# Projecting fourteen blocks among the first layer's gathers, building the first block's cells ahead of pass 1, and spreading the read-back of a table

## The reference

```
edge_index = stack([src, dst])
x = layernorm(x + L0(x, edge_index, weight, attn_l, attn_r))   # attention over 4 heads
x = layernorm(x + L1(x, L1_W, edge_index))                     # h = x @ W;  sum of d[src] d[dst] h[src]
x = layernorm(x + L2(x, edge_index, edge_weight, W1, b1, W2, b2))  # two such layers, weighted
x = layernorm(x + L3(x, W, edge_index))                        # h = x @ W.T
# L0: alpha = softmax(leaky_relu(alpha_l + alpha_r)); out = sum over heads of alpha * (x @ weight)[dst]
```

## Time and profile before

| | |
|---|---|
| median of three runs | 3285.67 us (3281.23 to 3291.87) |
| profiled execution, its own time | 3282.31 us, span 3280.5 us |
| gather loop and preparations | 0 to 151.7 us |
| first table | to 223.4 us, first gather of pass 1 at 227.37 us |
| pass 1 | 230.3 to 1364.7 us (first and last product of a chunk) |
| PE, DVE, ACT, POOL busy | 94%, 69%, 54%, 60% of the span |
| granted clock of PE, mean | 0.977 |

### The profile page before, as it was taken

The page is one execution under the profiler, slowest core; times in us unless marked ns, Lnnn a source line. Parts: engine busy times, 40 slices in busy tenths (PEclk is TensorE's granted clock), DMA queues, the critical chain, the costliest instruction groups (busy, mean ns, idle before and its releaser), DMA issues.

```text
span 3280.5 us, 58762 instructions
## 1 busy us (share of the span) xinstructions
PE 3072.6 (94%) x18902; PEld 2516.0 (77%) x18902; DVE 2278.6 (69%) x8972; ACT 1770.7 (54%) x4797; POOL 1974.7 (60%) x1952
## 2 busy tenths in 40 slices
PE   6788999999999997799999999899999998999998
PEld 5666777777877776578888887788888876888887
DVE  6668999999999997477777777466666673322333
ACT  3555878878878876444444444344444453232222
POOL 6627777777777776577777777577777770000000
PEclk9888999999999998899999999899999999999999
DMA  6246878878877878667767665766767666444443
GB/s 204 76 178 197 256 239 251 256 244 255 260 243 248 260 244 275 222 200 219 212 214 213 209 213 173 265 215 212 214 211 216 211 198 218 159 153 137 156 170 119
DMA packets 338323, 690.01 MB, mean 210 GB/s; under 512 B 61814, under 2 KB 185532, under 8 KB 337114
## 3 DMA queue, kind: packets, MB, share of 16 engines
q1 hardware_dynamic: 244506, 433.77, 39.1%
q0 software_dynamic: 91568, 250.58, 27.0%
q10 hardware_dynamic: 1936, 1.84, 0.2%
HBM read 495.15 MB, written 190.82 MB: 209 GB/s over the span
## 4 chain that ended last, share of the span: by engine, by line
PE 71%; DVE 10%; DMA 10%; POOL 3%; ACT 3%; issue 2%; SPq 1%; ACTq 0%; DVEq 0%
PE PS L2100 24%; PE PS L2177 15%; PE PS L2146 7%; DMA G<-T,idx 6%; PE PS L2148 6%; PE PS L2054 4%; PE PS L1895 2%; POOL G L2248 2%; PE PS L2027 2%; PE PS L1896 2%; PE PS L2078 2%; DVE soh L1481 2%; PE PS L2114 1%; DVE M L1363 1%; DVE R L1372 1%
## 5 line engine op out<-in xcount | busy, mean ns | idle before, releaser
L2248 POOL DMA_INDIRECT G<-T,idx x1800 | 1853.5, 1030 | 639.3 <-issue 257.5
L2100 PE MATMUL PS<-H,aw 128*128 128x256 f32 x4214 | 1078.5, 382 | 12.3 <-DMA aw<-AW 8.0
L2100 PEld LDWEIGHTS PS<-H,aw 128*128 128x128 f32 x4214 | 789.7, 191 | 129.0 <-issue 8.8
L1723 ACT ACTIVATE R<-G,wD 128x256 fp32r<-128x256 f32 x990 | 500.4, 508 | 699.7 <-PE PS L2148 482.4
L1372 DVE SCALAR_TENSOR_TENSOR R<-G,wD,R 128x256 fp32r<-128x256 f32 x990 | 480.6, 485 | 373.3 <-ACT R L1723 369.3
L2148 PE MATMUL PS<-R,Mr 128*128 128x512 f32 x990 | 575.6, 583 | 24.1 <-DVE R L1372 22.7
L2146 PE MATMUL PS<-G,M 128*128 128x257 f32 x1620 | 522.0, 406 | 48.6 <-DMA G<-T,idx 44.7
L2177 PE MATMUL PS<-HH,cr 128*128 128x512 f32 x2205 | 501.4, 389 | 0.4 <-DVE cr L1560 0.3
L2177 PEld LDWEIGHTS PS<-HH,cr 128*128 128x128 f32 x2205 | 413.3, 188 | 88.4 <-DVE cr L1560 2.6
L1781 ACT CAST atp<-PS 128x512 bf16<-128x512 f32 x588 | 336.2, 575 | 123.7 <-PE PS L2027 95.7
L2146 PEld LDWEIGHTS PS<-G,M 128*128 128x128 f32 x1620 | 266.0, 194 | 84.4 <-DMA G<-T,idx 32.1
(11 more groups left out here) (252 smaller groups left out, 3980.6 us busy)
## 6 DMA issues: line engine op xcount, KB each, us to landing
aw<-AW SPq DMA_DIRECT2D x301, 448.0 KB, 3.6
AT<-atp SPq DMA_DIRECT2D x539, 128.0 KB
br<-AT SPq DMA_DIRECT2D x77, 896.0 KB, 4.8
AW<-awp SPq DMA_DIRECT2D x264, 256.0 KB
G<-T,idx POOLq DMA_INDIRECT x1800
AT<-atf SPq DMA_DIRECT2D x49, 256.0 KB
T<-tst SPq DMA_DIRECT2D x96, 128.0 KB
H<-T SPq DMA_DIRECT2D x12, 896.0 KB, 12.0
```

Of the source, the lines that this page charges most:

```text
L1723: e.activation(R[m % NR][:, 0:D], G[slot][:, 0:D], ACT.Copy, scale=wD[:, k // NC, k % NC:k % NC + 1]).then_inc(s_rw, 1)
L2100: ins = e.matmul(ps, aw[n_ % NAW][:, s_ % 7, :], H[:, s_, :], start=s_ == 0, stop=s_ == NBK - 1)
L2248: e.indirect_dma_start(G[slot][:, 0:D], None, TAB[p][0:N, :], bass.IndirectOffsetOnAxis(ap=idx[:, block_of(p, k), k % NC:k % NC + 1], axis ...
```

## The change

It has three parts. (1) In the gather loop, from iteration 28 on, fourteen of the 49 blocks (`AMONG`) are turned and projected among the gathers, in six slots for turned tiles (two are lent from `counts1`) instead of four. The first five products (`NRAW`) come before `d1` is known, so ACT stores them unscaled and scales them at iterations 38 to 42 (`scale`). Counters of turns and products are now looked up (`TURN0`, `PRODUCT0`). The windows, digits and degrees sit two to twelve iterations earlier; a fifth group is early (five groups, 35 blocks), and 14 blocks are `LATE`; POOL normalizes 14 blocks instead of 10. (2) The cell sort of the first built block leaves pass 1: DVE has it (`BUILD0`) behind its first-layer work, PE and ACT around the last projections; `FIRST_PAIR` falls from 28 to 6, so pairs are spread over 798 chunks instead of 776, and the sort of the second block starts at chunk 0. (3) The six reloads with a due chunk had 739, 739, 739, 739, 739 and 755; now they have 738, 750, 762, 774, 786 and 798.

```diff
-PERM, FIRST_PAIR, LAST_PAIR = 9, 28, 6
+PERM, FIRST_PAIR, LAST_PAIR = 9, 6, 6
-ROW_AT, WINDOW_AT, TURN_AT = 3, 8, (14, 15, 16)
-DIGIT_AT = (22, 23, 24, 25, 26, 27, 28)
-DEGREE_AT, ROOT_AT = 37, 44
-EARLY_AT = ((7, 14, 18), (24, 36, 39), (37, 43, 46), (45, 48, 48))
+ROW_AT, WINDOW_AT, TURN_AT = 3, 8, (11, 12, 13)
+DIGIT_AT = (20, 21, 22, 23, 24, 25, 26)
+DEGREE_AT, ROOT_AT = 31, 32
+EARLY_AT = ((7, 14, 18), (20, 32, 34), (33, 39, 44), (34, 44, None), (39, None, None))
+AMONG = {28 + 10 * x // 7: x for x in range(14)}
+NRAW, SCALE_AT = 5, 38
...
-SHARED = list(LATE)[1::2]
+BEHIND = [g for g, at_ in enumerate(EARLY_AT) if at_[2] is None]
+SHARED = list(range(GROUPS[BEHIND[0]], NBK))[1::2]
...
-    ready = [(0, b) for b in range(LATE[0])]
+    ready = [(0, b) for b in range(len(AMONG), LATE[0])]
...
+    S_ += [(0, ("build", "dup", 0)), (k - 7, ("build", "totals", 0)), (k + 9, ("build", "cells", 0))]
+    T_ += [(k - 8, ("build", "totals", 0)), (k - 5, ("build", "rank", 0))] + [(k + 8, ("build", "permute", 0, c)) for c in range(NC)]
...
+BUILD0 = [("cellhot", 0), ("pieces",), ("pick", 0), ("pack", 0), ("over", 0), ("less", 0), ("slots", 0), ("load", 0),
+          *(("place", 0, c) for c in range(NC))]
...
             early_group(1, 1)
-            digit_sums(NBK // DB - 1)
             early_group(2, 0)
-            early_group(1, 2)
-            early_group(2, 1)
             w.wait_ge(s_ds, 1)
...
+            early_group(1, 2)
             w.wait_ge(s_sqd, 1)
             for i in range(4):
                 newton("d1n", i, d1[:, :], degI[:, :], [t_[:, :] for t_ in rt])
...
+            early_group(3, 0)
+            early_group(2, 1)
+            early_group(4, 0)
             early_group(3, 1)
+            early_group(2, 2)
+            early_group(4, 1)
             early_group(3, 2)
-            for _, step in FIRST[EARLY][0]:
+            for _, step in FIRST[EARLY][0][:16]:
+                first(step)
+            early_group(4, 2)
+            for _, step in FIRST[EARLY][0][16:]:
                 first(step)
...
+            for step in BUILD0:
+                behind_(step)
             for p in (1, 2, 3):
                 aggregate(p)
...
                 if b >= 1:
                     first_rows(b - 1)
+                if b - 1 in AMONG:
+                    follow(0, ("multiply", AMONG[b - 1]))
+                if b in AMONG:
+                    follow(0, ("turn", AMONG[b]))
...
+            free = UNITS1[-1][-1] + 4
+            reload_at = [max(free + r * (chunks_of(1) - free) // 6, *(stored[b] + 4 for b in blocks_in(r))) for r in range(6)]
...
-                                         + [(max(UNITS1[-1][-1], *(stored[b] for b in blocks_in(r))) + 4, (reload2, r)) for r in range(6)]):
+                                         + [(reload_at[r], (reload2, r)) for r in range(6)]):
```

More of the change, by code:

```diff
@@ L157, in follow_late @@
         k = put("soft", EARLY, i)
-    S_.append((k + 1, ("exp", EARLY)))
+    S_.append((4, ("exp", EARLY)))
+    for n, g in enumerate(BEHIND):
+        if EARLY_AT[g][1] is None:
+            S_.append((8, ("root", g)))
+        S_ += [(9 + 18 * n + 3 * i, ("normalize", b)) for i, b in enumerate(range(GROUPS[g], GROUPS[g + 1])) if b not in SHARED]
     for i in range(3, 6):
         put("soft", EARLY, i)
-    ready = [(0, b) for b in range(LATE[0])]
+    ready = [(0, b) for b in range(len(AMONG), LATE[0])]
     stages = ("mul", "mix", "sum", "stat", "aggr")
@@ L201, in first_early, with first_order @@
     for g, (e, r, n) in enumerate(EARLY_AT):
-        out[r].append(("root", g))
+        if r is not None:
+            out[r].append(("root", g))
         out[e].append(("exp", g))
-        for i, b in enumerate(range(GROUPS[g], GROUPS[g + 1])):
-            out[min(n + i, NBK - 1)].append(("normalize", b))
+        if n is not None:
+            for i, b in enumerate(range(GROUPS[g], GROUPS[g + 1])):
+                out[min(n + i, NBK - 1)].append(("normalize", b))
+    for b in range(NRAW):
+        out[SCALE_AT + b].append(("scale", b))
     return out
 FIRST_EARLY = first_early()
+def first_order():
+    turns, products = [], []
+    for b in range(NBK):
+        turns += [("edge", 2 * b), ("edge", 2 * b + 1)]
+        if b >= 1:
+            products.append(("rows", b - 1))
+        if b - 1 in AMONG:
+            products.append(("table", AMONG[b - 1]))
+        if b in AMONG:
+            turns.append(("table", AMONG[b]))
+    products.append(("rows", NBK - 1))
+    for _, (kind, b, *_) in FIRST[EARLY][2]:
+        if kind != "build":
+            (turns if kind == "turn" else products).append(("table", b))
+    return turns, products
+TURNS0, PRODUCTS0 = first_order()
+TURN0, PRODUCT0 = ({x: i for i, x in enumerate(order)} for order in (TURNS0, PRODUCTS0))
+NX0 = 6
 def chunks_of(p):
@@ L1656, in first @@
             def first(step):
-                kind, b = step
-                if kind == "exp":
+                kind, b = step[0:2]
+                if kind == "build":
+                    behind_(step[1:])
+                elif kind == "exp":
                     w.wait_ge(s_v, at["soft", b, 2])
@@ L1825, in aggregate @@
                     follow(p, step)
+            for _, step in FIRST[EARLY][1]:
+                first(step)
+            w.wait_ge(s_wt, 1)
+            w.wait_ge(s_pj, PRODUCT0["rows", NBK - 1] + 1)
+            e.copy(W4[:, 0, 0:D], PT[:, 0:D])
+            e.copy(W4[:, 1, 0:D], PA[1][:, 0:D]).then_inc(s_w4, 1)
             for p in (1, 2, 3):
@@ L2161, in aggregate @@
                     follow(p, step)
+            for _, step in FIRST[EARLY][2]:
+                if step[0] == "build":
+                    behind_(step[1:])
+                else:
+                    follow(0, step)
+            w.wait_ge(L["W4"], 16)
+            w.wait_ge(s_xt, turn_at(2, 0))
+            for i in range(2):
+                for j in range(2):
+                    ins = e.transpose((PT, PA[1])[i][:, j * P:(j + 1) * P], W4r[:, j, i * P:(i + 1) * P], ident[:, :])
+            ins.then_inc(s_wt, 1)
             for p in (1, 2, 3):
```

141 lines of the change are left out of this document (75 added, 66 removed).

## The result

The changed kernel takes 3265.85 us (median of 12 runs, 3261.0 to 3276.6), the kernel before 3284.82 in the same comparison; the ratio is 0.9953 with a 95% interval of 0.9938 to 0.9968. So it is faster, but by 19 us between the medians, and by 15 (10 to 20) by the ratio, where 43 were forecast, and the time lies just outside the range of 3220 to 3264. In three of the six comparisons of this document every kernel took 13 to 15 per cent longer (the kernel before 3712 to 3763 us instead of 3279 to 3285), so times and stages are set beside each other only at the same level. The profiled execution took 3262.61 us with a span of 3260.8.

A forecast was written before the change was run, and what follows sets the result against it. PE, busy 94% of the span, was taken as the bound, so only its idle or waiting stretches could give time. 3282.3 - 20 - 15 - 6 = 3241 us, with the runs' median 3.4 higher; stated as 3242, range 3220 to 3264.

The forecast's parts named there:

- PE needs 21 x 1.71 = 35.9: Gather loop from iteration 28 to 48: PE's own work at 1.71 us an iteration, 35.9 us.
- 15.1 us for the blocks: Gather loop: PE's work for the 14 blocks moved in, 14 x 1.08 us.
- My 4.4 us for the clock: Gather loop: 51 us of PE work take 4.4 us more at a clock of 0.92.
- The waits were forecast at 7.6: Gather loop: 5.6 us for turns waiting on ACT and 2 us for ACT's table switches.
- my bound of 168: Latest loop end, if every table switch and a whole trip to ACT count; 160 us was forecast.
- Rival C: In the loop ACT waits for DVE at iterations 39 and 44; loop ends at 172, total 3254 us; chance 0.10.
- 22 chunks of 1.350 instead of 1.25 us: Start of pass 1, chunks 6 to 27: each goes from the gather's pace to 1.350 us with pairs there.
- rival B: Parts 1 and 3 act, but pass 1's pace isn't set by the build: 3261 us; chance 0.10.
- half of 3 each: End of pass 1: six single reloads cost between 0 and 18 us, taken as 9, against 15.4 before.
- rival D: Spreading the reloads gives nothing back, six stalls of 3 us; 32 us gained in all, 3252 us; chance 0.05.
- Rival F: Slower: late DVE results hold up ACT's queue in the loop; 3290 us if DVE is 48 us late; chance 0.05.
- E: Total within 0.3%, if part 1 is lost in the loop and one other part too; chance 0.05.

The follow-up runs named there:

- rows_half_2: Changed kernel without the second wide product of first_rows in loop iterations 28 to 48, at the shorter times: 3255.2 us, ratio 0.9930 to the kernel before.
- the second comparison: Changed kernel, unedited, measured again against the kernel before at 3281.7 us: 3267.5 us, ratio 0.9967.
- pair17: Changed kernel with FIRST_PAIR 17 instead of 6: ratio 0.9960 to the kernel before, which took 3711.9 us there.

## Why the prediction was wrong

**Part 1, 20 us forecast, 6.3 measured.** The step that failed is "PE needs 21 x 1.71 = 35.9". The 1.71 us were the distance of two turns in one place, in which PE did nothing else and ran at full clock; the row that counts is the window of the same 54.1 us, in which PE was busy 47.44 us, 2.26 an iteration. Split in two, that window of the kernel before shows a start at half clock:

```profile
97.60:106.30 8.70, 8.65 (x47) 7.88 (x48) 8.70 (x28) 2.00 (x8) 6.71 (x7) 0.50 0.35 106
106.30:151.70 45.40, 38.79 (x255) 33.69 (x254) 25.92 (x94) 30.94 (x97) 35.72 (x61) 1.00 0.32 96
```

The rest of the difference is, as far as it is known, some 3 us of products for the digits and degrees and a 22nd group of products in the window; about 3 us are not accounted for. With the 15.1 us for the blocks 47.44 makes 62.5, and the changed kernel shows 62.88. My 4.4 us for the clock made up part of it; 35.9 + 15.1 + 4.4 = 55.4 was 7 short. The waits were forecast at 7.6 and came to 72.5 - 62.9 = 9.6. So the loop ended at 170.1, beyond my bound of 168. Behind the loop 47.6 us passed instead of 43.6: PE was busy 43.66 there, just the forecast, and the 3.9 us of idle time, the 2.04 us wait for ACT among them, were not in it. The 4.0 us from the last block to the first gather held.

One sum over the rows would have stopped the forecast: from 97.6 to 223.4 us PE did 47.44 + 0.31 + 57.82 = 105.6 us of work, which the change only moves. An end at 203.6 left PE 0.4 us of idle time in the whole stretch. In fact its idle time went from 20.2 to 13.6 us (120.1 less 62.9 and 43.7) and its busy time from 105.6 to 106.5, which makes the 5.7 us by which the stretch is shorter. That PE's work is what the forecast lacked agrees with rows_half_2, where less of it made the loop shorter.

Rival C had the loop's end nearly right (172) and the cause wrong. ACT came to iteration 39 straight from a normalize, without a wait for DVE; PE waited for the two table loads. From the rows of iteration 38 to those of 39 it took 6.1 us, where its neighbours took 2.5 to 4.1, and it took the same 6.1 us in rows_half_2 with less work for PE. The loads were 1.28 us each, and the activations followed 10 and 20 ns behind: no drain here either, where the Trainium skill ("ScalarE: Activation LUTs", What ACT_TABLE_LOAD costs) has 1.38 us.

**Part 2, 15 forecast, 6.9 measured.** Two terms were mis-sized. The start was put at 22 chunks of 1.350 instead of 1.25 us and 2 us for the sorts, 4 in all: it costs 7.2. The pace behind it was nearly right, so rival B is out: behind chunk 50 a chunk takes 14.1 / 685 = 0.021 us less where I had 0.025. But over 685 chunks that is 14.1 us for 17.1, and the last 75 chunks, whose share of the forecast was 2, lie in the stage that is read for part 3. At the start DVE was busy 21.2 of 35.7 us before; the first pairs and the sorts of the next blocks fill it to 34.1, and the chunks fall behind the gathers' pace. That DVE is what holds them is read from this share and not tested by an edit of DVE's work; pair17, with fewer pairs there, is in line with it. PE's clock went from 0.74 to 0.99 in this window, with no gain in time.

**Part 3, 6 forecast, 5.1 measured.** The size was met, and luck had a hand in it: "half of 3 each" for the six single reloads was a choice between 0 and 18 us. The cost of the burst at its place (9.5 and 12.7 us in the two pairs) is what the rows said. What remains of it further on differs from pair to pair, 8.5 us and nothing, so neither the sum of the forecast nor rival D's (spreading gives nothing back) is shown. The Trainium skill ("DMA: Bandwidth & Descriptors", Issuing engines are not separate DMA queues) has all transfers on the same 16 engines, whoever issues them; the pair in which nothing remains agrees with that, the pair with 8.5 us does not bear it out. One reading for rival D was wrong: the window with a DMA share of 1.00 does not show that one reload alone fills the 16 engines. At 343 GB/s its 10 us hold 3.4 MB, of which the reload is 0.9; the others are gathers and stores. Rival F did not come about; E, a gain within 0.3%, lies outside the first interval (0.9938 to 0.9968) but not outside that of the second comparison (0.9948 to 0.9987).

The sign was right. Part 1 fell out of its own bounds (12 to 28), which came from the same count of PE's work as the term; part 2 lay within its bounds (-3 to 28) and part 3 too (-3 to 15), but the range took in only one of them at a time. There is also a slip in the sum: 3282.3 - 41 + 3.4 is 3244.7, not 3242, which changes nothing here.

## What to carry to other kernels

Before forecasting that a stretch shrinks by moving work, add up the bound engine's busy time in the windows that the move spans: what is left to gain is its idle time there, here 20.2 us, of which 6.6 were won; work that moves from a low clock to a high one can add to that (three blocks took 5.8 us instead of 3.3). A hole in the trace may be worth less than its length, if the engines behind it catch up; in one of three profiles here they made up 8 us of 12.7, in the others none. So follow one counter (here the k-th chunk) through both traces to a point well behind the hole, and in more than one pair of profiles, before pricing it. And where an engine has slack at a stage's start, ask whether the work moved there leaves it any.

## What the runs showed of the hardware

The kernel before ran at 3279 to 3285 us in three comparisons and at 3712 to 3763 in the other three, on one chip (number 8) at 3281.7 and at 3711.9. At the longer times POOL issued 515 gathers from 350 to 1200 us instead of 622, and PE's granted clock was 0.96 instead of 1.00, but PE's busy time fell by 89 us: engines stood idle. The longest waits named "issue" of PE, with one of POOL, in that window of the changed kernel at 3733 us, and then the longest one of PE where it takes 3267; "issue" is time in which the engine waited for nothing that the profile shows:

```profile
PEld PS L2091 <- issue: 53.3, 66, 4.0
PEld PS L2118 <- issue: 43.9, 61, 3.7
...
PE PS L2091 <- issue: 33.0, 43, 3.2
POOL G L2323 <- remote: 28.4, 28, 1.8
```

```profile
PEld PS L2210 <- issue: 6.2, 11, 1.2
```

What holds the engines' own instruction streams up there was not found. The changed kernel gains 0.0075 of the time at this level (0.9925, 0.9902 to 0.9948) and 0.0033 to 0.0047 at the other; the intervals touch, so that it gains more here is not shown. But the loop without 9.2 us of PE's work was 5.7 us shorter at one level and no shorter at the other, so an edit that takes work from one engine should be judged at both.
